# Windowed attention and gated layers of a decoder in one stage, batches interleaved, no stop between the two layers

## The chip, the cores and the metric

One NeuronCore of one Trainium2 chip runs the whole kernel. The metric is the device time of one execution in microseconds. The engines are PE (TensorE, matmuls and transposes), DVE (VectorE), ACT (ScalarE), POOL (GpSimd) and SP, which here only issues DMAs. Each takes its instructions in order; semaphores connect them.

## The reference, cut to what matters

The kernel computes a decoder on x (4 batches of 512 tokens, 256 channels): an RWKV layer, a quantised cross attention, a mixture of experts, a linear attention, a cross attention, and at the end two layers of windowed attention with a gated layer. Each of these blocks adds its result to x and normalises. The change is in the last block alone:

```python
def _layer(x, wqkv, qs, ksc, wo, lg, lb, w1, b1, w2, b2):
    h = shift_token(x)                     # second half of the channels comes from the token before
    q, k, v = jnp.split(h @ wqkv, 3, axis=-1)        # 8 heads of 64
    q = l2norm(q) * qs
    k = l2norm(k) * ksc
    q, k = rotary_xpos(q, k)
    o = local_attention(q, k, v)           # 128 queries see their own and the previous 128 keys
    x = x + o @ wo
    h = shift_token(x)
    h = (h - mu) / jnp.sqrt(var + 1e-05) * lg + lb
    a, g = jnp.split(h @ w1 + b1, 2, axis=-1)        # 682 hidden channels each
    return x + (a * gelu(g)) @ w2 + b2
x = _layernorm(x + layer1(layer0(x)))
```

## The kernel before, in words

`windowed` runs four stages one after another: attention of layer 0, gated layer 0, attention 1, gated layer 1. Each is a function that reserves its SBUF tiles and semaphores, makes a plan (a list of steps in one order), and then writes each engine's instructions by walking through that same plan. So the plan is the order of work on every engine. Between stages stands `settle`: every engine, SP too, waits for the last step of the stage.

**Attention** (`windowed_plan`, `attention_sp`, `attention_pe`, `attention_dve`, `attention_act`, `attention_pool`). A unit u is two windows of 128 tokens; a layer has 8 units, 16 windows (numbered 0 to 15 in this text, four to a batch). Weights and activations are split into a high and a low bf16 part, and a product takes three passes. Steps of a unit:

- `split`: ACT casts x, DVE shifts it by one token, POOL makes the low parts (L3034).
- `project`: 6 matmuls of 512 columns for q, k or v of a window (L2774); ACT copies the result out (L2972) and squares q and k (L2978); DVE sums the squares (L2875). `invert`: ACT takes the root (L2982), DVE the reciprocal.
- `rotate`: POOL multiplies by the sine (L3045, L3046), DVE by the cosine, adds POOL's part and multiplies by the norm (L2893, L2896, L2899). `turn`: 4 transposes on PE (L2783), a copy on ACT.
- `score`: mask products and q times k into banks 0 to 3 (L2795, L2802). `softmax`: DVE takes maxima (L2910), ACT the exponentials (L3008, which empties the banks), DVE the reciprocal sums and the weighting (L2916, L2919), each in two halves of four heads.
- `flip`: transposes of the weights (L2814), copied by DVE and ACT in turn (L2944). `combine`: weights times v (L2829), copy on ACT (L3020). `output`: times wo (L2839), DVE adds to x (L2930).

The plan puts the rotations of unit u+1 and the projections of unit u+2 among the scores, softmaxes, flips, combines and outputs of unit u. The first window of a batch looks at 128 keys only (`alone`), so its score, softmax and flips are half as large.

**Gated layer** (`ffn_plan`, `ffn_sp`, `ffn_pe`, `ffn_dve`, `ffn_act`, `ffn_pool`). The unit is a batch g. `normalise`: PE shifts the tokens (L3118, L3119), DVE takes statistics and scales (L3174, L3188), ACT the root (L3233); POOL adds the bias b2, and in layer 1 the x kept from the block's start, to x_tok (L3283, L3288). `transpose`: PE, then ACT scales (L3248), DVE makes high and low parts (L3198, L3200). `first`, six hidden tiles ft: 12 matmuls into two banks, value and gate (L3140); ACT gelu of the gate (L3257), DVE value times gate (L3209), ACT high part (L3262), POOL low part (L3304). `second`, two halves: 36 matmuls each (L3154), DVE adds to x_tok (L3217). `split1`, `split2` split w1 and w2 on ACT and POOL (L3237, L3241, L3292, L3296). At the end of layer 0, `channels` turns x into channel order for the next attention; in layer 1, `norm` is the final layer norm, and SP stores each batch.

All PSUM uses other than scores take banks 4 to 7 in rotation, in the order of the plan. A use waits until the one four uses before it is emptied:

```python
self.empty = m.emptied[bank], m.uses[bank]
...
use.update(m.banks(steps, (4, 5, 6, 7)))
```

## Time and profile before

| | us |
|---|---|
| median of 3 runs | 2854.57 (2853.91 to 2859.57) |
| profiled execution, its own time | 2848.74 |
| its span | 2847.4 |
| busy in the span: PE / DVE / ACT / POOL | 2229.3 / 1674.0 / 1182.0 / 566.6 |

The span is the time from the first to the last instruction in the profile; the execution's own time lies 1.3 us above it. Mean granted TensorE clock 0.876. The windowed block is the last 891 us. The page's forty slices of the span (71 us each) show it in the last twelve and a half:

```profile
PE   6993589896408999287589999995888697788678
...
DVE  4666965568763333466556565643777642677663
ACT  2222844345232333132225555553665442566442
POOL 2110000001363554401200000001222141322052
PEclk9996789998658999589689999997899898899999
```

### The profile page before, as it was taken

To read this page: it belongs to the slowest core of one execution; us is meant where nothing else is said; L and a number is where in the kernel's file an instruction comes from. 1 tells how busy PE (TensorE), PEld (TensorE's weight loads), DVE (VectorE), ACT (ScalarE), POOL (GpSimd) and SP (SyncE) were. 2 spreads that over 40 slices of the span, in tenths; PEclk is the share of its full clock that TensorE was granted. 3 is DMA by queue.
4 is the path that set the end of the run, shared out by engine and by line. 5 is a ranking of instruction groups with operands and counts; after the bars stand their busy time and mean duration, and the time that the engine had idled before them with its cause. 6 is when DMAs were issued, how large, how long until landed. Compare 5 with 4: busy or idle time off the path is not lost. (4 is left out here: it accounts for less than half of the span.)

```text
span 2847.4 us, 41664 instructions
## 1 busy us (share of the span) xinstructions
PE 2229.3 (78%) x15694; PEld 1432.6 (50%) x15694; DVE 1674.0 (59%) x3413; ACT 1182.0 (42%) x2185; POOL 566.6 (20%) x489
## 2 busy tenths in 40 slices
PE   6993589896408999287589999995888697788678
PEld 3552157573306888144235555653555444455534
DVE  4666965568763333466556565643777642677663
ACT  2222844345232333132225555553665442566442
POOL 2110000001363554401200000001222141322052
PEclk9996789998658999589689999997899898899999
DMA  3005000100360111323311111102000001000000
GB/s 109 1 1 155 14 1 1 45 1 1 96 215 26 46 46 38 108 65 79 102 48 36 24 36 24 24 13 88 1 1 1 11 1 59 1 1 1 36 12 23
DMA packets 75074, 113.30 MB, mean 40 GB/s; under 512 B 22916, under 2 KB 59744, under 8 KB 74208
## 3 DMA queue, kind: packets, MB, share of 16 engines
q1 hardware_dynamic: 71808, 102.24, 12.0%
q0 software_dynamic: 3072, 8.39, 0.9%
q8 instruction: 131, 2.15, 0.3%
q14 instruction: 63, 0.52, 0.1%
HBM read 85.38 MB, written 31.20 MB: 41 GB/s over the span
## 5 line engine op out<-in xcount | busy, mean ns | idle before, releaser
L2479 DVE TENSOR_REDUCE xa_max<-psum 128x1 f32<-128x1024 f32 (+1 forms) x256 | 248.8, 988 | 144.7 <-PE psum L2382 144.1
L2575 ACT ACTIVATE xa_work<-psum 128x1024 f32<-128x1024 f32 (+1 forms) x208 | 212.9, 1024 | 202.1 <-PE psum L2405 200.5
L2420 PE MATMUL psum<-xa_work,xa_values 128*33 128x128 f32 (+1 forms) x3328 | 232.1, 284 | 0.0
L2420 PEld LDWEIGHTS psum<-xa_work,xa_values 128*33 128x33 f32 (+1 forms) x3328 | 172.9, 114 | 78.9 <-issue 73.7
L2774 PE MATMUL psum<-wqkv_l,x_hl_l 128*128 128x512 bf16 x576 | 146.1, 401 | 60.6 <-POOL x_hl_l L3034 32.4
L3140 PE MATMUL psum<-h_ch_f,w_f 128*128 128x512 bf16 (+1 forms) x576 | 139.3, 400 | 32.1 <-DVE h_ch_f L3200 9.5
L1645 DVE TENSOR_SCALAR moe_raw<-psum,tile_b 128x256 f32<-128x256 f32 x184 | 78.3, 474 | 139.3 <-PE psum L1487 138.2
L2405 PE MATMUL psum<-xa_query_rows,xa_key_rows 98*128 98x512 bf16 (+1 forms) x416 | 131.5, 399 | 8.4 <-ACT xa_work L2575 7.7
L1741 POOL TENSOR_TENSOR x_ch<-moe_raw,x_ch 128x512 bf16<-128x512 f32 x92 | 105.5, 1158 | 149.9 <-ACT x_ch L1701 147.8
L1487 PE MATMUL psum<-moe_rows,moe_w 128*128 128x256 bf16 x1104 | 132.9, 279 | 3.0 <-POOL moe_rows L1737 3.0
L2382 PE MATMUL psum<-xa_key_rows,xa_query_rows 96*128 96x512 bf16 (+1 forms) x512 | 129.4, 348 | 6.7 <-DVE xa_max L2479 3.0
L1498 PE MATMUL psum<-moe_w,x_ch 128*128 x1104 | 130.2, 280 | 0.0
L3008 ACT ACTIVATE w_p_l<-psum,w_max_l 128x256 f32<-128x256 f32 (+1 forms) x256 | 110.6, 458 | 28.8 <-DVE w_max_l L2912 28.6
L2774 PEld LDWEIGHTS psum<-wqkv_l,x_hl_l 128*128 128x128 bf16 x576 | 56.0, 102 | 130.3 <-issue 48.6
L1487 PEld LDWEIGHTS psum<-moe_rows,moe_w 128*128 x1104 | 110.0, 100 | 18.8 <-issue 4.2
L1498 PEld LDWEIGHTS psum<-moe_w,x_ch 128*128 128x128 bf16 x1104 | 110.9, 101 | 16.7 <-issue 1.3
L3140 PEld LDWEIGHTS psum<-h_ch_f,w_f 128*128 128x128 bf16 (+1 forms) x576 | 56.8, 102 | 111.4 <-issue 33.9
L1038 PE MATMUL psum<-ctx_f,query_sum 128*128 128x512 f32 (+1 forms) x256 | 105.5, 538 | 7.9 <-DVE query_sum L1090 7.9
L3045 POOL TENSOR_TENSOR qk_other_l<-qk_raw_l,rotary_l 128x256 f32<-128x256 f32 x64 | 64.7, 1011 | 196.0 <-DVE qk_rot_l L2896 196.0
L1059 PE MATMUL psum<-ctx_f,probs_t_bn 128*128 128x128 f32 (+1 forms) x832 | 100.0, 277 | 2.8 <-DVE probs_t_bn L1116 2.8
L1701 ACT CAST x_ch<-moe_raw 128x512 bf16<-128x512 f32 x92 | 56.9, 618 | 101.4 <-DVE moe_raw L1645 101.4
L1174 POOL TENSOR_TENSOR x_tok<-x_tok,rows 128x4096 f32<-128x4096 f32 x1 | 8.8, 8809 | 451.5 <-DVE fused L1135 451.5
(439 smaller groups left out, 4832.2 us busy)
## 6 DMA issues: line engine op xcount, KB each, us to landing
xa_key_rows<-cross_keys SPq DMA_DIRECT2D x48, 200.1 KB, 3.5
moe_raw<-in_moe_w SPq DMA_DIRECT2D x16, 512.0 KB, 5.2
x_ch<-in_moe_w SPq DMA_DIRECT2D x16, 512.0 KB, 4.8
moe_rows<-slots_in SPq DMA_DIRECT2D x23, 256.0 KB, 2.8
slots_out<-moe_rows SPq DMA_DIRECT2D x23, 256.0 KB, 2.1
ctx_f<-in_ctxT SPq DMA_DIRECT2D x2, 2401.5 KB, 21.5
cross_keys<-xa_k_hl SPq DMA_DIRECT2D x6, 800.5 KB, 3.7
xa_query_rows<-cross_queries SPq DMA_DIRECT2D x48, 64.0 KB, 3.5
```

The lines of the kernel that those rows point to most:

```text
L1038: ins = pe.matmul(u.wide[:, c0 - a:c1 - a], t["qsum"][:, n * P:(n + 1) * P], t["keys"][:, b * S2 + c0:b * S2 + c1], start=True, stop=True)
L1487: ins = pe.matmul(u.ap[:, a * SLOT:(a + 1) * SLOT], w1[:, w, h, cf], t["x"][j % 2][:, x, h, :], start=(h, k) == (0, 0), stop=(h, k) == (1, 2))
L1498: ins = pe.matmul(u.ap[:, a * D:(a + 1) * D], t["hidden"][j % 2][:, x, f, q], w2[:, w, f, :], start=(f, k) == (0, 0), stop=(f, k) == (7, 2))
L1741: g.tensor_tensor(hidden[:, 1, f, :], t["act"][n % 2], hidden[:, 0, f, :], ALU.subtract).then_inc(*s.h_low.up())
L2382: ins = pe.matmul(u.wide[:, x - c0:y - c0], t["q_rows"][n % 3][0:SPLIT, a, qt * P:(qt + 1) * P], t["k_rows"][n % 3][0:SPLIT, a, x:y], star ...
L2405: ins = pe.matmul(u.wide[0:rows, a * T:(a + 1) * T], t["k_rows"][n % 3][:, a, kt * P:kt * P + rows], t["q_rows"][n % 3][:, a, :], start=Tr ...
L2420: ins = pe.matmul(total.ap[a * LANE:a * LANE + VC, c:c + PIECE], t["v"][b][0:rows, kt, first + a, :], exps[0:rows, a, c:c + PIECE], start= ...
L2479: v.tensor_reduce(t["maxes"][n % 2][:, qt * HU + a, part:part + 1], u.wide[:, 0:c1 - c0], AX.X, ALU.max).then_inc(*u.free)
L2575: act.activation(t["exps"][k % EXPS][0:rows], u.wide[0:rows].rearrange("p (m q) -> p m q", q=T), ACT.Exp, scale=1.0 / float(np.sqrt(np.flo ...
L2774: ins = pe.matmul(b.ap, x[:, i, h, w * P:(w + 1) * P], t["wqkv"][:, j, h, cols], start=(h, n) == (0, 0), stop=(h, n) == (1, 2))
L3008: ins = act.activation(t["p"][n % 2][:, i, lo:2 * P], scores[:, i, :], ACT.Exp, bias=t["peak"][n % 2][:, i:i + 1], scale=8.0, accum_out=t[ ...
L3140: ins = pe.matmul(u.ap[0:rows, :], t["w1"][:, y, h, o:o + rows], t["h_ch"][g % 2][:, x, h, :], start=(h, n) == (0, 0), stop=(h, n) == (1, 2))
```

## The change

The four stages of the block become one, with one plan of 545 steps for both layers.

- Units count on through both layers (0 to 15), batches too (g 0 to 7). `windowed_sp` walks the plan too.
- Gated steps of batch g (0 to 2 in a layer) stand among the windows of the next batches: `normalise` in window 4(g+1)+1, `root`, `scaled` and `transpose` in +2, hidden tiles 0 to 2 in +3, 3 to 5 in +4, `second` in +5, `channels` (layer 1: `stat`, `root_last`, `final`) in +6. So batch 0's are windows 5 to 10, batch 1's 9 to 14, batch 2's begin with window 13. What is not placed by window 15 comes after it, then batch 3. In layer 0 this rest is interleaved with `prologue(UPL)`: split, projections and rotations of layer 1's first unit and projections of its second.
- The weights of layer 1 are loaded by `fetch` steps: wqkv into the two buffers of raw q and k once the last units have read them, the rotary table, wo, w1, w2 as their readers finish. `weigh` and `tables` split and scale them.
- SBUF: one set of tiles for both layers. w_pt goes from two buffers to one, w_v from five to four, w_p from two buffers of eight heads to three of four heads, h_ch and hidden from two to one, h_act from three to two. The normalised tokens (h_tok before) are written into x_ch, in the batch's own part, which the attention has read by then; in layer 1 the kept x is loaded there, batch by batch. h_f32 and w_oc lie in the rows tile, raw w1 and w2 in the room of hidden and h_act.
- `normalise` copies the shifted half out of PSUM (DVE), and the scaling reads the copy. Semaphores of finals and statistics count once a batch.
- The first wqkv cast waits for its own half only.

The core of the diff:

```diff
+    early, late = {}, {}
+    for layer in range(2):
+        w0, g0 = layer * TILES, layer * B
+        late[w0] = [("split1", layer, 0)]
+        late[w0 + 1] = [("split1", layer, 1)]
+        late[w0 + 2] = [("split2", layer, n) for n in range(2)]
+        for g in range(g0, g0 + B - 1):
+            w = w0 + TPB * (g - g0 + 1)
+            for at, where, steps in ((1, late, [("normalise", g)]), (2, early, [("root", g), ("scaled", g)]), (2, late, [("transpose", g)]),
+                                     (3, early, firsts(g, 0, 3)), (4, early, firsts(g, 3, HT)), (5, early, seconds(g)[:1]),
+                                     (5, late, seconds(g)[1:]), (6, late, close(g))):
+                if w + at < w0 + TILES:
+                    where.setdefault(w + at, [])
+                    where[w + at] = where[w + at] + steps
+    swap = {TILES - 4: [("fetch", "wqkv", 0)], TILES - 2: [("fetch", "wqkv", 1), ("fetch", "tab", 1)]}
+    for w, steps in ((TILES - 3, [("weigh", 0)]), (TILES - 1, [("weigh", 1), ("tables", 1)])):
+        late[w] = late.get(w, []) + steps
+    plan, tail, last = prologue(0), [], []
+    for layer in range(2):
+        for u in range(layer * UPL, (layer + 1) * UPL):
+            main = []
+            for w in range(WU):
+                n = WU * u + w
+                main += swap.get(n, []) + [("score", u, w)] + tail[0:1] + [("softmax", u, w)] + early.get(n, []) + tail[1:2] + last
+                main += late.get(n, [])
+                last, tail = tail[2:], [("flip", u, w), ("combine", u, w), ("output", u, w)]
+            rotations = rotate(u + 1) if (u + 1) % UPL else []
+            projections = project(u + 2) if (u + 2) % UPL > 1 else []
+            plan += mingle(main, mingle(rotations, projections))
+        g = B * layer + B - 1
+        main = last + tail[0:1] + firsts(g - 1, 3, 4) + tail[1:2] + firsts(g - 1, 4, HT) + tail[2:] + [("fetch", "wo", 1)] * (1 - layer)
+        main += seconds(g - 1)[:1] + [("normalise", g)] + seconds(g - 1)[1:] + [("root", g), ("scaled", g)] + close(g - 1)[:1]
+        main += [("transpose", g)] + firsts(g, 0, 2) + close(g - 1)[1:2] + firsts(g, 2, HT - 1) + close(g - 1)[2:] + firsts(g, HT - 1, HT)
+        main += seconds(g) + [("fetch", "w1", 1), ("fetch", "w2", 1)] * (1 - layer) + close(g)
+        plan += main if layer else mingle(main, prologue(UPL))
+        last, tail = [], []
+    return plan
...
-                 v=ring("w_v", 5, [P, WU, INNER]), p=ring("w_p", 2, [P, HL, 2 * P]), pt=ring("w_pt", 2, [P, HL, 2, P]),
+                 v=ring("w_v", 4, [P, WU, INNER]), p=ring("w_p", 3, [P, 4, 2 * P]), pt=sb("w_pt", [P, HL, 2, P]),
...
-        settle(m, [use["output", UNITS_W - 1, WU - 1].done])
...
+            if what == "wqkv":
+                sp.wait_ge(*s.swung(4 * (UPL - 1 + h)))
+                sp.wait_ge(*s.swapped(4 * (UPL - 1 + h)))
+                sp.wait_ge(*s.squared(WU * (UPL - 1 + h)))
+                fetch_wqkv(1, h)
...
+        elif kind == "normalise":
+            b, x, late, st = use[step], batch_tokens(m, u), late_tokens(m, u), t["stats"]
+            v.wait_ge(*s.in_low(HALVES * WU * (u + 1)))
+            v.wait_ge(*b.full)
+            v.tensor_copy(late[:, :, :, P:D], b.ap.rearrange("p (h q d) -> p h q d", h=HALVES, q=2)).then_inc(*b.free)
...
+        elif kind == "first":
+            ft, = step[2:]
+            n, rows = HT * u + ft, hidden_rows(ft)
+            a, b = use[step + (0,)], use[step + (1,)]
+            if n > 1:
+                v.wait_ge(*s.h_low(n - 1))
...
+            act.wait_ge(*b.full)
+            act.activation(t["gate"][n % 2][0:rows, :], b.ap[0:rows, :], ACT.Gelu,
+                           bias=m.col("b1g", HT * (u // B) + ft, rows)).then_inc(*b.free)
+            if ft == 0 and u:
+                act.wait_ge(*use["second", u - 1, 1].full)
+            act.wait_ge(*a.done)
+            act.copy(t["hidden"][0:rows, 0, ft, :], t["act"][n % 2][0:rows, :]).then_inc(*s.h_high.up())
```

The order that results for windows 7 and 8 of layer 0 (numbers as in the code: u, w, then which or tile):

```
score(3,1) turn(4,0,0) flip(3,0) split(6) softmax(3,1) turn(4,0,1) first(0,0) project(5,1,1) first(0,1) turn(4,1,0) first(0,2) project(5,1,2) combine(3,0) turn(4,1,1) output(2,1) invert(5)
score(4,0) rotate(5,0,0) flip(3,1) project(6,0,0) softmax(4,0) rotate(5,0,1) first(0,3) project(6,0,1) first(0,4) rotate(5,1,0) first(0,5) project(6,0,2) combine(3,1) rotate(5,1,1) output(3,0) project(6,1,0)
```

## Rows read from the trace of the kernel before

**Rows 1.** Windows view: us, busy us (count) of PE, PEld, DVE, ACT, POOL; clock; DMA; GB/s.

```profile
1956.50:2256.00 299.50, 228.90 (x1600) 153.80 (x1600) 204.01 (x417) 166.36 (x435) 67.57 (x80) 0.88 0.06 21
2256.00:2398.50 142.50, 120.06 (x657) 65.32 (x656) 59.82 (x137) 52.03 (x74) 46.25 (x32) 0.93 0.02 6
...
2697.50:2847.40 149.90, 115.77 (x624) 61.35 (x622) 74.87 (x184) 57.00 (x79) 55.52 (x36) 0.92 0.09 33
2079.60:2234.50 154.90, 126.41 (x937) 89.56 (x936) 113.62 (x234) 91.17 (x249) 32.20 (x38) 0.91 0.00 1
```

**Rows 2.** PE timeline: start us, us, work; the mask products that open a score.

```profile
2079.58 1.91 PE L2795 MATMUL psum<-mask_b_l,ident_b_l 128*128 128x512 bf16 x4
...
2113.21 1.89 PE L2795 MATMUL psum<-mask_b_l,ident_b_l 128*128 128x512 bf16 x4
...
2130.22 0.60 PE L2795 MATMUL psum<-mask_b_l,ident_b_l 128*128 128x256 bf16 x4
...
2234.51 0.59 PE L2795 MATMUL psum<-mask_b_l,ident_b_l 128*128 128x512 bf16 x2
...
2446.64 0.60 PE L2795 MATMUL psum<-mask_b_l,ident_b_l 128*128 128x256 bf16 x4
...
2522.08 1.03 PE L2795 MATMUL psum<-mask_b_l,ident_b_l 128*128 128x512 bf16 x4
...
2675.01 0.59 PE L2795 MATMUL psum<-mask_b_l,ident_b_l 128*128 128x512 bf16 x2
```

**Rows 3.** Groups by line and form, 1970 to 2398.5 us.

```profile
L2774 PE MATMUL psum<-wqkv_l,x_hl_l 128*128 128x512 bf16 x288 | 72.8, 400 | 30.2 <-POOL x_hl_l L3034 16.4 <-ACT qk_raw_l L2972 9.6 <-ACT w_k_l L2991 3.0
L3140 PE MATMUL psum<-h_ch_f,w_f 128*128 128x512 bf16 x240 | 59.0, 405 | 12.8 <-issue 4.7 <-DVE h_ch_f L3200 4.6 <-DVE h_tok_f L3188 2.7
L3008 ACT ACTIVATE w_p_l<-psum,w_max_l 128x256 f32<-128x256 f32 x96 | 44.0, 485 | 13.0 <-DVE w_max_l L2912 13.0
...
L3045 POOL TENSOR_TENSOR qk_other_l<-qk_raw_l,rotary_l 128x256 f32<-128x256 f32 x32 | 32.4, 1011 | 99.2 <-DVE qk_rot_l L2896 99.2
...
L2910 DVE TENSOR_REDUCE w_max_l<-psum 128x4 f32<-128x1024 f32 x24 | 29.2, 1217 | 0.0
L3154 PE MATMUL psum<-w_f,hidden_f 128*128 128x256 bf16 x240 | 28.9, 273 | 0.0
...
L2893 DVE TENSOR_TENSOR qk_rot_l<-qk_raw_l,rotary_l 128x512 f32<-128x512 f32 x32 | 23.3, 728 | 0.0
L3304 POOL TENSOR_TENSOR hidden_f<-h_act_f,hidden_f 128x512 bf16<-128x512 f32 x20 | 23.1, 1157 | 51.3 <-ACT hidden_f L3262 51.3
...
L2944 DVE COPY w_pt_l<-psum 128x512 f32<-128x512 f32 x28 | 18.8, 686 | 11.0 <-PE psum L2814 10.4
...
L3209 DVE SCALAR_TENSOR_TENSOR h_act_f<-psum,cols,gelu_f 128x512 f32<-128x512 f32 x20 | 15.0, 749 | 39.4 <-ACT gelu_f L3257 35.9 <-issue 3.5
L3257 ACT ACTIVATE gelu_f<-psum,cols 128x512 f32<-128x512 f32 x20 | 13.8, 688 | 36.4 <-PE psum L3140 36.3
...
L3262 ACT CAST hidden_f<-h_act_f 128x512 bf16<-128x512 f32 x20 | 12.3, 618 | 18.3 <-DVE h_act_f L3209 18.3
```

**Rows 4.** Timeline of ScalarE: a table load and the exponential behind it.

```profile
2106.31 1.28 ACT L3008 ACT_TABLE_LOAD   x1 [2.75 <-DVE w_max_l L2912]
...
2107.61 0.47 ACT L3008 ACTIVATE w_p_l<-psum,w_max_l 128x256 f32<-128x256 f32 x1
```

**Rows 5.** PE timeline: an output step after idle time, and one without.

```profile
2092.78 3.62 PE L2839 MATMUL psum<-wo_l,w_oc_l 128*128 128x256 f32 x8 [2.76 <-ACT qk_raw_l L2972]
...
2107.32 1.89 PE L2839 MATMUL psum<-wo_l,w_oc_l 128*128 128x256 f32 x8
```

**Rows 6.** Timeline: GpSimd's weight split and the same VectorE subtraction beside it and alone.

```profile
2267.45 2.95 POOL L3292 TENSOR_TENSOR w_f<-w_f,w_f 128x1364 bf16<-128x1364 f32 x1
...
2267.81 3.13 DVE L3200 TENSOR_TENSOR h_ch_f<-h_f_f,h_ch_f 128x512 bf16<-128x512 f32 x1
...
2289.23 0.69 DVE L3200 TENSOR_TENSOR h_ch_f<-h_f_f,h_ch_f 128x512 bf16<-128x512 f32 x1
```

More of the change, by code:

```diff
@@ L2662, in rotate @@
         return steps + [("turn",) + o for o in order[-LAG:]]
-    plan = [("split", 0)] + project(0) + rotate(0) + project(1)
-    tail, last = [], []
-    for u in range(UNITS_W):
-        main = []
-        for w in range(WU):
-            main += [("score", u, w)] + tail[0:1] + [("softmax", u, w)] + tail[1:2] + last
-            last, tail = tail[2:], [("flip", u, w), ("combine", u, w), ("output", u, w)]
-        rotations = rotate(u + 1) if u + 1 < UNITS_W else []
-        projections = project(u + 2) if u + 2 < UNITS_W else []
-        plan += mingle(main, mingle(rotations, projections))
@@ L2674, in windowed_plan, with firsts, seconds, close @@
-    return plan + last + tail
+    def firsts(g, a, b):
+        return [("first", g, ft) for ft in range(a, b)]
+    def seconds(g):
+        return [("second", g, 0), ("second", g, 1)]
+    def close(g):
+        return [("channels", g)] if g < B else [("stat", g), ("root_last", g), ("final", g)]
+    def prologue(u):
+        return [("split", u)] + project(u) + rotate(u) + project(u + 1)
+    early, late = {}, {}
[12 more added lines that the diff above has]
+                    where[w + at] = where[w + at] + steps
@@ L2716, in windowed_attention @@
         for p in plan:
-            if p[0] in ("project", "turn", "combine", "output"):
+            if p[0] in ("project", "turn", "combine", "output", "normalise", "second"):
                 steps.append(p)
@@ L2720, in windowed_attention @@
                 steps += [p + (g,) for g in range(len(flips(*p[1:])))]
+            elif p[0] in ("transpose", "first", "channels"):
+                steps += [p + (i,) for i in range(2)]
             elif p[0] == "score":
@@ L2862, in attention_dve @@
         if kind == "split":
-            c0, first = u * WU * P, alone(u, 0)
+            c0, first = u % UPL * WU * P, alone(u, 0)
             if u:
                 v.wait_ge(*s.in_low(HALVES * u))
+            if u >= UPL:
+                for h in range(HALVES):
+                    v.wait_ge(*use["channels", (u - UPL) // WU, h].done)
             if first:
@@ L2954, in attention_act @@
         if kind == "split":
-            c0 = u * WU * P
+            c0 = u % UPL * WU * P
+            if u >= UPL:
+                for h in range(HALVES):
+                    act.wait_ge(*use["channels", (u - UPL) // WU, h].done)
             if u > 1:
@@ L3305, in ffn_pool @@
+            n, rows = HT * u + ft, hidden_rows(ft)
+            if ft == 0 and u:
+                g.wait_ge(*use["second", u - 1, 1].full)
+            g.wait_ge(*s.h_high(n + 1))
+            g.tensor_tensor(t["hidden"][0:rows, 1, ft, :], t["act"][n % 2][0:rows, :], t["hidden"][0:rows, 0, ft, :],
                             ALU.subtract).then_inc(*s.h_low.up())
```

629 lines of the change are left out of this document (320 added, 309 removed).

## The prediction, made blind

> **What bounds it now.** I read the stages first [rows 1]: of the 2847.4 us span the windowed part takes 890.9 us, from 1956.5 on. Attention of layer 0 lasts 299.5 us with TensorE (PE) busy for 228.9, its gated layer 142.5 with 120.1; layer 1 repeats the pair and ends with 149.9 for the gated layer, PE busy for 115.8. PE is the busiest engine in each and is idle for about 200 us in all, so filling that is the prize. Then I read the starts of the scores [rows 2], which cut attention into windows: each layer has 16, and windows 5 to 14 of layer 0 last 154.9 us (2079.58 to 2234.51), PE busy for 126.4 of them [rows 1]. From the score of window 15 to the first score of layer 1 there are 212.1 us (2234.51 to 2446.64): the attention tail, the gated layer, the stop and the start-up of layer 1. In layer 1 windows 5 to 14 take 152.9 us (2522.08 to 2675.01) and window 15 and the gated layer 172.4, to the end of the span.
>
> **What the change does.** No product is taken out. It moves, per layer, the gated steps of two batches, and the first half of the hidden tiles of a third, into windows 5 to 15; the rest of that batch and the last one come after window 15, in layer 0 interleaved with layer 1's start-up. In a cycle of four windows: D (7, 11, 15) gets three hidden tiles, A (8, 12) the other three, B (9, 13) both output products and the next normalise, C (6, 10, 14) root, scaling, transposes, channels. Price of the moved work on PE at full rate: a hidden tile is 12 matmuls. The mean of 405 ns in [rows 3] is latency, not spacing; 288 such matmuls are 72.8 us busy, 0.25 each, and steady groups come every 0.22, so a tile is 2.7 us. Half an output product is 36 matmuls at 0.12 (28.9 us for 240), 4.4 us. A normalise is 2 us, a transpose pair 1. For windows 5 to 14 that makes 12 tiles 32.2, 4 halves 17.6, the rest 10: 60 us. If nothing else stood in the way these windows would last 215 us or less.
>
> **Why I don't take 215.** All engines run in order and the moved steps share banks 4 to 7, in rotation, with the attention. I walked each window, with the durations of [rows 3]. Window 7, t=0 at the end of its score: PE turns and flips to 2.5; VectorE (DVE) copies two flip banks (0.69 each) to 3.2 and takes the first maximum (1.22, then 0.2 for the scaling) to 4.6; ScalarE (ACT) loads its table (1.28) [rows 4] and does eight exponentials at 0.47, to 9.7; DVE finishes weighting at 11.0. Meanwhile PE does a turn, tile 0 and a projection, to 7.1. Tile 1 then needs the turn's bank, which ACT copies only behind the exponentials, at 10.3: 3.2 us idle. Its second half needs the bank of tile 0's value, free after table load, gelu (0.69) and DVE's product (0.75), at 13.05. So it goes on: ACT's cast of a tile (0.62) waits for DVE's product, and every copy behind it waits too. The next score ends at 26.4 (it is a half-size one), against 17.0 measured [rows 2]. Window 8: tile 4's second half waits from 8.7 to 13.4, because DVE has the softmax and a rotation ahead of tile 3's product; then a POOL rotation (1.01+0.77) stands behind tile 4's low half (1.16) on GpSimd, DVE waits for it, tile 5's product behind that, and the output behind its ACT copy. 29 us, with the half-size softmax. The others in the same way. 9: the 4.4 us products stand where PE used to wait, 23.6. 10: DVE's list sets it (softmax to 12.7, rotation 14.8, scaling of the batch 18.2, rotation 20.3, a sum of squares, then the output's addition at 21.9, whose bank the transposes need), 25.7. 11: as 7 with one projection more, 27.7. 12: as 8 without projections; tile 5 waits for tile 3's product until 14.1, 23. 13: bound by PE, 19.8. 14: the output waits for its copy behind exponentials and root (10.2), the transposes for the scaling (13), 17. 5: the normalise on top of today's, 19.5. 6: the transposes wait for the scaling at 16, 21.2. Together 232.9 us. By the same walk today's window 7 is 15.5, where the rows say 17.0; so I add 1.5 per window: **248 us**, +93 against 154.9. The clock is one reason for the 1.5: after 2.76 us without work eight output matmuls took 3.62 us, elsewhere 1.89 [rows 5]; the mean granted clock of these windows is 0.91 of 2.4 GHz, so part of them ran at 1.2 [rows 1].
>
> **The border.** From the end of window 15's score: hidden tiles of batch 2 with flips, combine and outputs to 22.6, new weights and tables split on ACT and DVE beside it (their loads are issued two windows earlier, and SP has only waits ahead of them that are met by then), first projection at 26, second half of output product at 54.4. Then scaling of batch 3 stands on DVE behind rotations: PE idle for about 12 us until its transposes and casts are done at 69.9, then 35 us of tiles, projections and products; first score of layer 1 at 108. With the 2.8 of window 15's score that is 110.8 against 212.1: **-101.3 us**. This is the real gain: 14.5 us of weight loads, the latency of the gated layer's start and the start-up's idle time are covered.
>
> **The end of layer 1.** Same front; no start-up to mix in. Batch 2's products end at 47.2, transposes at 52.2, tiles 56 to 72.2, then 3.7 us idle for the last tile's gelu, product, cast and low half, products to 84.7, and statistics, scaling and store as today (7.5): 92, with some slow clock 95, and 2.8 for the score: 97.8 against 172.4, **-74.6 us**. But windows 5 to 14 of layer 1 cost 248 too, plus about 4.3 for the final normalisation on DVE in windows 10 and 14, against 152.9: **+99.4 us**.
>
> **Small edits.** Splitting w1 and w2 moves into windows 0 to 2: four ACT copies behind exponentials, four GpSimd subtractions. While such a one ran, a DVE subtraction with two SBUF inputs took 3.13 us instead of 0.69 [rows 6]. Bounds 0 and 10 us a layer; I take 4, since a rotation or two meets them: +8. The rings that shrink (w_pt to one, w_v to four, hidden and h_ch to one) cost 0: each is read out a window before it is written again, by PE's order of steps; if a combine were late by a window, the flip copies would wait for it, some 2 us each. Fetching batches of kept x on SP, one 0.5 MB load each, 0: the first reader, GpSimd, has a window until its next rotation. Waiting for each half of wqkv apart lets the first cast start earlier: -1.4. Table loads: counted over both orders of steps, 61 against 45; the walks have them in.
>
> **Sum:** 93 - 101.3 + 99.4 - 74.6 + 8 - 1.4 = +23 us. The profiled execution took 2848.7 us (span 2847.4); the median shown is 2854.6, 5.8 more. On the median: **2877.7 us**.
>
> **A rule beside the rows.** In [rows 4] a load takes 1.28 us and the exponential starts 0.02 later. The Trainium skill, ScalarE: Activation LUTs, What ACT_TABLE_LOAD costs, adds about 1.38 us of drain to each switch; by that the 16 extra loads would cost 22 us more, 2900 in place of 2878. The trace shows no such gap here, so I leave it out.
>
> **Rivals.** (1) *PE-bound filling, faster.* The tiles fit into today's waits because ACT and DVE reach them earlier than I walked; windows 5 to 14 then cost the 60 us of PE work alone: 33 less per layer, 66 in all, 2812; with half of today's 28 us of idle time filled as well, 2784. For it: ACT is busy for 91 and DVE for 114 of 154.9 us [rows 1], neither is full. Against it: order, not load, makes the waits. 0.36 for the whole side. (2) *GpSimd against DVE.* The 12 to 15 low halves (1.16 each) and bias additions of each layer now run beside rotations, which read two SBUF inputs. Some 52 us of GpSimd work in both layers; if each blocks DVE as in [rows 6] (2.44 of 2.95 us), +41: 2919. The Trainium skill, SBUF — State Buffer, Who interferes with whom, calls this an exclusive lock held for a whole instruction; the trace agrees with its 3.13 us. It decides if it hits DVE while PE waits for it. 0.12. (3) *The stop stays.* If layer 1's weight split (on ACT and DVE, behind window 15's tiles) or its load is late, the first projection waits as today, about 14.5 us: 2892. 0.05. My forecast: 0.41. The rest, 0.06, is terms that cancel to near zero.
>
> **Chances.** A measurement of this kernel tells 0.2% (6 us) from nothing. Faster 0.36, same 0.06, slower 0.58. Range: down to 2797, which leaves the deep end of rival 1 out, up to 2925, which takes in rival 2. The likeliest case's own range is 2850 to 2905 (1.4 us per window either way).
>
> **What would show it.** Right: score starts 23 to 30 us apart in windows 7 to 12 where they are 11 to 21 apart now; PE waiting there for gelu, for the tile's product and for copies behind exponentials; about 110 us from layer 0's last score to layer 1's first; 98 us from the last score to the end; some 60 table loads. Wrong: windows 5 to 14 in 215 us or less per layer (rival 1); rotations on DVE well above 0.73 us (rival 2); a hole of PE over 10 us before the first projection of layer 1 (rival 3).

## The result and the profile after

The changed kernel takes 2892.07 us (median of 4 runs, 2885.68 to 2895.47) against 2855.36 for the kernel before on the same chip: ratio 1.0123, 95% interval 1.0103 to 1.0144. The forecast was 2877.7, in a range of 2797 to 2925: the direction was right, the size some 14 us short (36.7 us slower in the medians, where 23 was forecast). The profiled execution shown here was the slowest of the four (2895.47, span 2894.2), and the one of the kernel before (2848.74) was faster than all its other runs, so the two profiles differ by 10 us more than the medians.

The windows view of the changed kernel, cut at the score starts: windows 0 to 4, windows 5 to 14, the border (score of window 15 to the first score of layer 1), the same three for layer 1, its last being the end. Columns as in [rows 1].

```profile
2005.60:2090.80 85.20, 64.85 (x425) 43.30 (x431) 61.97 (x121) 52.37 (x135) 31.54 (x30) 0.86 0.00 1
2090.80:2336.60 245.80, 188.70 (x1271) 123.80 (x1283) 154.44 (x338) 130.33 (x302) 51.64 (x55) 0.91 0.03 9
2336.60:2454.80 118.20, 93.75 (x538) 54.37 (x545) 50.75 (x98) 47.30 (x84) 29.43 (x30) 0.91 0.04 11
2454.80:2541.50 86.70, 63.89 (x425) 42.81 (x431) 62.03 (x122) 53.36 (x136) 30.32 (x29) 0.86 0.05 17
2541.50:2788.80 247.30, 190.89 (x1255) 122.33 (x1266) 159.39 (x354) 127.48 (x299) 56.77 (x57) 0.89 0.03 7
2788.80:2894.20 105.40, 77.09 (x436) 44.31 (x439) 41.32 (x102) 35.49 (x61) 21.50 (x16) 0.87 0.08 25
```

The stage of the kernel before, in the same cut, in two of its rows (windows 0 to 4 and the border of layer 0; windows 5 to 14 stand in [rows 1]):

```profile
2003.00:2079.60 76.60, 62.59 (x438) 40.37 (x437) 58.73 (x124) 49.39 (x133) 22.39 (x28) 0.91 0.00 1
2234.50:2446.60 212.10, 160.53 (x885) 89.33 (x884) 91.20 (x198) 79.10 (x132) 59.22 (x47) 0.88 0.06 24
```

So, between the same scores, in us:

| stretch | before | after | difference | forecast |
|---|---|---|---|---|
| to the first score | 2003.0 | 2005.6 | +2.6 | -1.4 |
| windows 0 to 4, layer 0 | 76.5 | 85.2 | +8.7 | +4 |
| windows 5 to 14, layer 0 | 154.9 | 245.8 | +90.9 | +93 |
| border | 212.1 | 118.2 | -93.9 | -101.3 |
| windows 0 to 4, layer 1 | 75.4 | 86.7 | +11.3 | +4 |
| windows 5 to 14, layer 1 | 152.9 | 247.4 | +94.5 | +99.4 |
| window 15 to the end | 172.4 | 105.4 | -67.0 | -74.6 |
| sum | | | +47 | +23 |

The spans differ by 46.8. Most of the first row is not the change's: the part of the program ahead of the stage is the same code, and its end lay up to 17 us apart between profiles (first score at 1993 to 2010 us), so everything below compares stretches, not spans. From the stage's first DMA to the first score it is 48.75 us before (1954.28 to 2003.03) and 48.21 after (1957.40 to 2005.61): the change takes 0.5 us off there, and the other 3.1 came from ahead of the stage. Two profiles of unaltered code differ by up to 2 us in a stretch, 4 in the end.

The reader should see two things in the first fence. In windows 5 to 14 PE is busy for 188.7 us where it was 126.4: 62 us more, close to the 60 of the forecast, which priced the moved work at full rate. But PE also idles 57.1 us there, where it idled 28.5. The holes were not filled, they doubled. And in windows 0 to 4 PE's work is unchanged while the stretch grew, with GpSimd busy for 31.5 us where it was 22.4.

**Inside window 7.** The timeline of the changed kernel, PE, ScalarE (ACT) and VectorE (DVE), from the softmax to the second half of tile 2 (the wait ahead of an instruction in brackets):

```profile
2144.82 1.28 ACT L3273 ACT_TABLE_LOAD   x1 [0.99 <-DVE w_max L3075]
2146.11 0.47 ACT L3273 ACTIVATE w_p<-psum,w_max 128x256 f32<-128x256 f32 x1
...
2149.72 0.63 ACT L3252 COPY w_k<-psum 128x512 f32<-128x512 f32 x1
2150.37 1.28 ACT L3323 ACT_TABLE_LOAD   x1
2150.41 4.57 PE L2986 MATMUL psum<-ff_ch,ff_w 128*128 128x512 bf16 x12 [4.16 <-ACT w_k L3252]
2151.66 0.69 ACT L3323 ACTIVATE ff_act<-psum,cols 128x512 f32<-128x512 f32 x1
2152.39 0.75 DVE L3142 SCALAR_TENSOR_TENSOR ff_act<-psum,cols,ff_act 128x512 f32<-128x512 f32 x1 [1.12 <-ACT ff_act L3323]
2153.17 0.62 ACT L3328 CAST ff_hidden<-ff_act 128x512 bf16<-128x512 f32 x1 [0.82 <-DVE ff_act L3142]
...
2157.38 1.47 PE L2986 MATMUL psum<-ff_ch,ff_w 128*128 128x512 bf16 x6 [0.67 <-DVE ff_act L3142]
```

This is the chain of the forecast step by step. The twelve matmuls at 2150.41 are tile 1: PE needs a bank whose copy (w_k) stands on ACT behind eight exponentials, and waits 4.16 us for it (walked, that is, worked out in the forecast: 3.2); then table load, gelu, product and cast of the tile before. After the wait the 12 matmuls take 4.57 us, against 2.7 at full rate. The forecast's second wait inside tile 1 doesn't show by itself: its bank is free at 2153.14, while the slow matmuls still run.

PE's groups in windows 5 to 14 of layer 0, changed kernel:

```profile
L2986 PE MATMUL psum<-ff_ch,ff_w 128*128 128x512 bf16 (+1 forms) x141 | 38.1, 422 | 19.0 <-DVE ff_act L3142 12.5 <-ACT w_k L3252 6.3
L2958 PE MATMUL psum<-wo,rows 128*128 128x256 f32 x80 | 22.9, 437 | 9.2 <-ACT w_k L3252 3.9 <-ACT w_q L3257 3.6 <-DVE ff_act L3142 0.9
L3000 PE MATMUL psum<-ff_w,ff_hidden 128*128 128x256 bf16 (+1 forms) x144 | 18.8, 284 | 0.0
...
L2973 PE MATMUL psum<-const,x_ch 128*128 128x128 f32 x24 | 5.9, 426 | 17.2 <-DVE x_ch L3121 11.3 <-DVE x_tok L3093 6.0
```

The gated layer's output products (`second`, L3000) wait for nothing. The hidden tiles (L2986) wait 19.0 us and the transposes (L2973) 17.2, for the tile's product, for copies behind exponentials, and for the scaling that stands on DVE behind softmax and rotations.

### The profile page after: what moved, and what is told of

Same layout as the page of the kernel before. It is cut to its first block and busy times, and to the rows that moved or that the text cites. A ratio compares the mean times of both kernels' runs of the same rounds, so it can differ in the third digit from the quotient of the medians.

```text
span 2894.2 us, 41751 instructions
## 1 busy us (share of the span) xinstructions
PE 2234.9 (77%) x15628; PEld 1441.2 (50%) x15694; DVE 1682.0 (58%) x3419; ACT 1202.5 (42%) x2201; POOL 562.2 (19%) x489
## 5 line engine op out<-in xcount | busy, mean ns | idle before, releaser
L2986 PE MATMUL psum<-ff_ch,ff_w 128*128 128x512 bf16 (+1 forms) x562 | 152.0, 426 | 60.4 <-DVE ff_act L3142 36.6
L2893 PE MATMUL psum<-wqkv,x_hl 128*128 128x512 bf16 x535 | 141.0, 404 | 35.3 <-POOL x_hl L3354 14.7
L2986 PEld LDWEIGHTS psum<-ff_ch,ff_w 128*128 128x128 bf16 (+1 forms) x576 | 59.4, 107 | 145.5 <-DVE ff_act L3142 45.5
L3273 ACT ACTIVATE w_p<-psum,w_max 128x256 f32<-128x256 f32 (+1 forms) x256 | 110.6, 458 | 15.6 <-DVE w_max L3075 15.4
L2893 PEld LDWEIGHTS psum<-wqkv,x_hl 128*128 128x128 bf16 x576 | 56.8, 103 | 104.4 <-issue 34.7
L3393 POOL TENSOR_TENSOR ff_hidden<-ff_act,ff_hidden 128x512 bf16<-128x512 f32 (+1 forms) x48 | 55.5, 1156 | 245.0 <-ACT ff_hidden L3328 245.0
L1059 PEld LDWEIGHTS psum<-ctx_f,probs_t_bn 128*128 128x128 f32 (+1 forms) x832 | 95.4, 192 | 3.4 <-DVE probs_t_bn L1116 3.4
```

The source lines that it names most:

```text
L1059: ins = pe.matmul(u.ap[:, 0:P], t["turned"][n % 2][0:rows, kt, :], t["values"][0:rows, n // TPB, kt, :], start=(kt == 0), stop=(kt == KT - 1))
L2893: ins = pe.matmul(b.ap, x[:, i, h, w * P:(w + 1) * P], t["wqkv"][:, j, h, cols], start=(h, n) == (0, 0), stop=(h, n) == (1, 2))
L2986: ins = pe.matmul(b.ap[0:rows, :], t["w1"][:, y, h, o:o + rows], t["h_ch"][:, x, h, :], start=(h, n) == (0, 0), stop=(h, n) == (1, 2))
L3273: ins = act.activation(t["p"][half % 3][:, i % 4, lo:2 * P], scores[:, i, :], ACT.Exp, bias=t["peak"][n % 2][:, i:i + 1], scale=8.0, accum ...
```

## The experiments

All durations are of windows views cut at score starts, as above. Every kernel ran on the same chip as the runs of the kernel before given with it.

### 1. One stage, but the gated layer behind the attention

The steps of batches are taken out of the windows, and run batch after batch behind window 15; in layer 0 all but batch 0 interleaved with layer 1's start-up. Buffers, code of each step and the splits among windows 0 to 2 stay as in the changed kernel.

```diff
-        for g in range(g0, g0 + B - 1):
-            w = w0 + TPB * (g - g0 + 1)
...
+        for g in range(g0, g0 + B):
...
+            part += (ready(g + 1) if more else []) + firsts(g, 3, HT) + ([("transpose", g + 1)] if more else []) + seconds(g)
...
-        plan += main if layer else mingle(main, prologue(UPL))
+            plan += main + rest[:cut] + mingle(rest[cut:], prologue(UPL))
```

> The changed kernel with no gated step inside the windows: all four batches' gated steps come after window 15, one batch after the other, in layer 0 interleaved with layer 1's start-up from batch 0's channels on. Same tiles, rings and weight loads. Theory 1 (the order of the moved steps among the attention, not the single stage, makes windows 5 to 14 long): they fall back from 246 and 247 us to 155 to 165 per layer; from layer 0's last score to layer 1's first it takes 185 to 200 us, the end 165 to 180; in all 2850 to 2875 us against 2892. Theory 2 (the single stage itself costs it: smaller rings, shared semaphores, x_ch reused): windows 5 to 14 stay above 200 us and the kernel stays above 2900.

Measured: 2865.29 us (2860.48 to 2866.97), before 2845.22, ratio 1.0070 (1.0046 to 1.0093).

```profile
1994.50:2082.30 87.80, 66.69 (x438) 43.83 (x437) 64.37 (x124) 52.73 (x136) 33.38 (x32) 0.86 0.00 1
2082.30:2235.50 153.20, 123.86 (x938) 88.45 (x937) 114.50 (x235) 92.68 (x251) 31.82 (x38) 0.93 0.04 15
2235.50:2435.20 199.70, 160.60 (x886) 89.39 (x885) 88.71 (x199) 76.44 (x130) 50.10 (x46) 0.91 0.02 7
...
2680.60:2859.20 178.60, 139.59 (x765) 78.25 (x763) 89.76 (x217) 61.22 (x103) 46.31 (x32) 0.90 0.08 24
```

Windows 5 to 14 return to 153.2 and 154.6 us. It is the gated steps among these windows, not the single stage and its buffers, that cost the 91 to 94 us. The border is 12.4 us shorter than before. That is the sum of several things: no stop, weights loaded ahead, the start-up mixed in, the splits gone from it, and another order of the gated steps. The end, which has no stop, got 6.2 us longer with the same order, so the single stage may be worth some 19 us in the border (an estimate, 12.4 and 6.2). Windows 0 to 4 stay long (87.8 and 90.8).

### 2. The cast of a tile later on ScalarE

The cast of each hidden tile is issued behind the next ACT step, so that its wait for DVE's product holds nothing up.

```diff
-            act.wait_ge(*a.done)
-            act.copy(t["hidden"][0:rows, 0, ft, :], t["act"][n % 2][0:rows, :]).then_inc(*s.h_high.up())
+            def cast(n=n, ft=ft, rows=rows, a=a):
...
+                pending.append(cast)
...
```

> The changed kernel with ScalarE's cast of a hidden tile (which waits for VectorE's product) put behind the next ScalarE step instead of right behind the gelu, except for a batch's last tile. If ScalarE standing in that cast's wait holds up the copies behind it, and with them the banks, windows 7, 8, 11 and 12 get 1 to 3 us shorter each and the kernel 8 to 20 us faster. If the value bank that waits for VectorE's product sets the pace, as the waits of PE say (36.6 us before the tile matmuls), under 5 us.

Measured: 2881.16 us in one run (before 2845.22); windows 5 to 14 take 245.9 and 248.7 us, no change beyond the 2 us spread. The forecast's remark that "every copy behind it waits too" is true in the timeline, and costs nothing that can be measured here. The end was 101.1, but experiment 5, whose casts stand as in the changed kernel, shows 101.3, so that is no gain either.

### 3. No table for gelu

Exp takes the place of Gelu in the hidden tiles, so those values are other ones; all else stays.

```diff
-            act.activation(t["gate"][n % 2][0:rows, :], b.ap[0:rows, :], ACT.Gelu,
+            act.activation(t["gate"][n % 2][0:rows, :], b.ap[0:rows, :], ACT.Exp,
```

> The changed kernel with Exp in the place of Gelu, so that this nonlinearity is another function than the reference's; nothing else differs. Exponentials and the gate share a table then: some 23 of 60 table loads go. If each such load (1.28 us) lies on the chain that sets a window, 20 to 30 us less. If the loads are hidden by other waits, under 8 us.

Measured: 2864.81 us in one run (before 2845.22). The table loads of ScalarE in the stage at the exponentials (L3273) and the gelu (L3323), changed kernel first, then this one:

```profile
L3273 ACT ACT_TABLE_LOAD x24 | 30.8, 1283 | 44.9 <-DVE w_max L3075 44.8
L3323 ACT ACT_TABLE_LOAD x13 | 16.7, 1283 | 17.6 <-PE psum L2986 17.4
```

```profile
L3273 ACT ACT_TABLE_LOAD x20 | 25.7, 1283 | 33.8 <-DVE w_max L3075 33.6
L3323 ACT ACT_TABLE_LOAD x3 | 3.8, 1283 | 17.6 <-PE psum L2986 17.6
```

Fourteen loads fewer, 60 to 46 in all (my expectation had counted on some 23). Windows 5 to 14 have six fewer each and take 236.8 and 238.5, 9.0 and 8.9 less: 1.5 us a load, with a spread of up to 2 us in each stretch. So nearly every load seems to lie on the path there, at about its own 1.28 us. With 2.66 us for each switch, the 1.28 and the 1.38 of drain that the Trainium skill states (ScalarE: Activation LUTs, What ACT_TABLE_LOAD costs), six on the path would have given 16 us; this run doesn't agree. Nor does the timeline of window 7 above: the copy of w_k ends at 2150.35, the load starts at 2150.37, and the gelu 0.01 us behind its end. The loads explain a tenth of the 91 us.

### 4. The smaller rings, on the kernel before

```diff
-                 v=ring("w_v", 5, [P, WU, INNER]), p=ring("w_p", 2, [P, HL, 2 * P]), pt=ring("w_pt", 2, [P, HL, 2, P]),
+                 v=ring("w_v", 4, [P, WU, INNER]), p=ring("w_p", 3, [P, 4, 2 * P]), pt=sb("w_pt", [P, HL, 2, P]),
...
```

> The kernel before with the changed kernel's attention rings alone: w_pt one buffer instead of two, w_v four instead of five, w_p three half buffers instead of two whole ones. The prediction took them at 0. If that holds, the span stays within 2 us of 2847 and windows 0 to 4 at 75 to 77 us a layer. If the rings are what makes windows 0 to 4 of the changed kernel last 85.2 and 86.7 us, they do so here: 8 to 10 us a layer, 16 to 40 us in all.

Measured: 2849.36 us in one run, before 2845.22. Windows 0 to 4 take 76.6 and 77.5 us, windows 5 to 14 154.8 and 154.1, border 212.1, end 172.6. Each is within 2.1 us of the kernel before; these three rings cost nothing, as priced. Those of the gated layer (h_ch, hidden, h_act) were not tried by themselves.

### 5. The changed kernel almost without the low splits

The low parts of w1 and w2 are made for eight columns of each piece only and no longer read (PE reads the high part in their place), so this part of the precision is left out. ScalarE's four casts stay.

```diff
-                        ins = pe.matmul(b.ap[0:rows, :], t["w1"][:, y, h, o:o + rows], t["h_ch"][:, x, h, :],
+                        ins = pe.matmul(b.ap[0:rows, :], t["w1"][:, 0, h, o:o + rows], t["h_ch"][:, x, h, :],
...
-            g.tensor_tensor(t["w1"][:, 1, h, :], t["w1_f32"][:, h, :], t["w1"][:, 0, h, :], ALU.subtract).then_inc(*s.w1_low.up())
+            g.tensor_tensor(t["w1"][:, 1, h, 0:8], t["w1_f32"][:, h, 0:8], t["w1"][:, 0, h, 0:8], ALU.subtract).then_inc(*s.w1_low.up())
...
```

> The changed kernel without the low parts of w1 and w2: GpSimd's four subtractions a layer are cut to 8 columns and the three passes of the gated products read the high part in their place, so that the number of matmuls is the same; the output lacks the low parts' share. If GpSimd against VectorE makes windows 0 to 4 long (85.2 and 86.7 us), they fall to 77 to 79. If the order of steps does, they stay above 82.

Measured: 2872.65 us in one run (before 2850.8). Windows 0 to 4 fall from 85.2 and 86.7 to 78.2 and 79.7, 7.0 in each layer; windows 5 to 14 stay (245.8 and 245.6). The collision in the changed kernel's timeline, then the group of the first rotation in windows 0 to 4 of layer 0, changed kernel:

```profile
2056.22 2.61 POOL L3377 TENSOR_TENSOR ff_w<-ff_act,ff_w 128x1280 bf16<-128x1280 f32 x1 [10.23 <-ACT ff_w L3301]
2056.89 2.48 DVE L3056 TENSOR_TENSOR qk_rot<-qk_raw,rotary 128x512 f32<-128x512 f32 x1
```

```profile
L3056 DVE TENSOR_TENSOR qk_rot<-qk_raw,rotary 128x512 f32<-128x512 f32 x10 | 10.8, 1079 | 0.0
```

and the same group in this experiment:

```profile
L3056 DVE TENSOR_TENSOR qk_rot<-qk_raw,rotary 128x512 f32<-128x512 f32 x10 | 7.3, 731 | 0.0
```

### 6. Two tiles a window, not three

```diff
-                                     (3, early, firsts(g, 0, 3)), (4, early, firsts(g, 3, HT)), (5, early, seconds(g)[:1]),
-                                     (5, late, seconds(g)[1:]), (6, late, close(g))):
+                                     (3, early, firsts(g, 0, 2)), (4, early, firsts(g, 2, 4)), (5, early, firsts(g, 4, HT)), (6, early, seconds(g)[:1]),
+                                     (6, late, seconds(g)[1:]), (7, late, close(g))):
...
```

> The changed kernel with two hidden tiles in each of three windows instead of three in two, output products and closing one window later. Three tiles in a row make PE wait twice for a value bank that VectorE frees only behind its softmax; two need all four banks once. By that theory windows 5 to 14 get shorter by 5 to 15 us a layer. If what counts is the number of windows with a table change and a broken-up softmax, they get longer, by 0 to 8 us a layer.

Measured: 2888.55 us in one run (before 2850.8), 37.8 us slower than before, as slow as the changed kernel. Windows 5 to 14: 244.0 and 243.6, 1.8 and 3.8 less, with batch 1's closing step now in window 15, behind them, and the border 1.4 longer; a miss for the theory that three tiles in a row are what hurts. The rival, that such windows get longer, is not borne out either. Spreading brings nothing that is clear of the spread.

### 7. Tiles ahead of the softmax

```diff
-                main += swap.get(n, []) + [("score", u, w)] + tail[0:1] + [("softmax", u, w)] + early.get(n, []) + tail[1:2] + last
+                main += swap.get(n, []) + [("score", u, w)] + tail[0:1] + [p for p in early.get(n, []) if p[0] == "first"] + [("softmax", u, w)] + [p for p in early.get(n, []) if p[0] != "first"] + tail[1:2] + last
```

> The changed kernel with one thing moved: in windows 7, 8, 11 and 12 the hidden tiles placed there stand ahead of the window's softmax on every engine, not behind it. Theory (a tile's bank and its product are held up because ScalarE and VectorE reach the gelu and the product only behind the exponentials and the weighting): the tiles run without those waits, PE waits for ff_act less than the 36.6 us of the changed kernel's stage, but the softmax, and with it the flips, come later; windows 5 to 14 change by -15 to 0 us per layer. Rival (the softmax chain itself sets these windows, so whatever is put ahead of it is added): windows 7, 8, 11 and 12 grow by 3 to 6 us each, windows 5 to 14 to 258 or more per layer.

Measured: 2887.6 us in one run (before 2850.57). PE's group of the hidden tiles over the whole stage, changed kernel, then this one:

```profile
L2986 PE MATMUL psum<-ff_ch,ff_w 128*128 128x512 bf16 (+1 forms) x562 | 152.0, 426 | 60.4 <-DVE ff_act L3142 36.6 <-ACT w_k L3252 9.9 <-DVE ff_ch L3133 6.5
```

```profile
L2986 PE MATMUL psum<-ff_ch,ff_w 128*128 128x512 bf16 (+1 forms) x561 | 134.7, 390 | 27.3 <-DVE ff_act L3142 14.0 <-DVE ff_ch L3133 6.5 <-issue 3.5
```

The tiles' waits fell by 33 us and their busy time by 17, and yet windows 5 to 14 took 243.2 and 245.2, only 2.6 and 2.2 less, and the kernel was as slow as the changed one (37.0 us above the kernel before). The wait has moved to the mask products that open the next score, which need the banks that the exponentials empty. Changed kernel, then this one:

```profile
L2914 PE MATMUL psum<-mask_b,ident_b 128*128 128x512 bf16 (+1 forms) x128 | 36.8, 416 | 6.4 <-ACT w_p L3273 6.4
```

```profile
L2914 PE MATMUL psum<-mask_b,ident_b 128*128 128x512 bf16 (+1 forms) x128 | 41.7, 447 | 38.3 <-ACT w_p L3273 38.3
```

Window 7 shrank from 27.7 to 23.5, window 8 grew from 26.7 to 32.7. The theory has the waits right, and the rival (258 us or more) is wrong in its size, but its reason holds in part: the tiles run freely, and what they save, the score behind the later softmax pays. The waits named in a group say where time is spent, not what it is worth to remove them.

### 8. Experiment 1 with the attention's own order

The splits had also changed how the attention steps are interleaved with projections and rotations. Here they are put in after the interleaving, so that the attention has exactly the order of the kernel before.

```diff
-        late[w0] = [("split1", layer, 0)]
-        late[w0 + 1] = [("split1", layer, 1)]
-        late[w0 + 2] = [("split2", layer, n) for n in range(2)]
...
+        for score, steps in ((("score", u, 1), [("split1", layer, 0)]), (("score", u + 1, 0), [("split1", layer, 1)]),
+                             (("score", u + 1, 1), [("split2", layer, n) for n in range(2)])):
...
```

> e1_serial_one_stage (no gated step in the windows) with the four weight-split steps put into the plan after the mingling, so that the attention's steps of windows 0 to 3 stand in exactly the order of the kernel before; the splits themselves stay in these windows. e1 took 87.8 and 90.8 us for windows 0 to 4 where the kernel before took 76.5 and 75.4. If the longer list has moved the turns, projections and rotations among each other and that costs it, windows 0 to 4 come back to 77 to 81 us, and the kernel is 15 to 25 us faster than e1 (2845 to 2852). If it is GpSimd's subtractions against VectorE, they stay at 86 or more.

Measured: 2861.78 us (2858.98 to 2869.45), before 2850.80, ratio 1.0039 (1.0025 to 1.0053). Windows 0 to 4: 85.5 and 87.1, where 77 to 81 was expected if the order is what costs, and 86 or more if GpSimd's subtractions are. The order is worth 2.3 and 3.7 us against experiment 1; the rest of their growth is elsewhere.

### 9. Experiment 8 with another order of gated steps

The next batch's normalise stands between this batch's hidden tiles rather than in front of all that are left, and the last batch's closing steps stand behind all hidden tiles, ahead of the output products.

```diff
-            if g > g0:
-                part += firsts(g, 0, 2) + close(g - 1)[:1] + firsts(g, 2, 3) + close(g - 1)[1:]
-            part += (ready(g + 1) if more else []) + firsts(g, 3, HT) + ([("transpose", g + 1)] if more else []) + seconds(g)
...
+            part += [norm] + firsts(g, 3, 4) if g == g0 else firsts(g, 0, 1) + [norm] + firsts(g, 1, 4)
+            part += [root, scaled] + firsts(g, 4, HT) + ([("transpose", g + 1)] if more else [])
+            part += (close(g - 1) if g > g0 else []) + seconds(g)
...
```

> e8_serial_order_kept with another order in the gated part: normalise of the next batch after the first hidden tile, root and scaling after the fourth, closing steps of the batch before in front of the output product. In e1 PE waited 4.05 us per batch for VectorE's product behind the scaling, and 2.5 to 3.5 us for the last low half. If that is the gated part's loss against the kernel before (178.6 us from the last score to the end, 172.4 there), the end falls by 6 to 14 us and the stretch from layer 0's last score to layer 1's first (199.7 in e1) by 4 to 12: then this version beats the kernel before by 5 to 20 us. If the single hidden buffer is what costs it, both stay within 3 us.

Measured: 2840.27 us (2836.86 to 2843.29), before 2850.80, ratio 0.9965 (0.9952 to 0.9977). The border falls from 199.6 to 184.5 us (4 to 12 less was expected), the end from 178.6 to 168.5. So the single hidden buffer, the rival of this expectation, is not what held them up.

### 10. Experiment 9 with the splits at windows 14 and 15

No rotation runs there, since the layer's last unit has been rotated.

```diff
-        for score, steps in ((("score", u, 1), [("split1", layer, 0)]), (("score", u + 1, 0), [("split1", layer, 1)]),
-                             (("score", u + 1, 1), [("split2", layer, n) for n in range(2)])):
-            at = plan.index(score)
+        for step, steps in ((("softmax", u + UPL - 1, 0), [("split1", layer, n) for n in range(2)]),
+                            (("softmax", u + UPL - 1, 1), [("split2", layer, n) for n in range(2)])):
+            at = plan.index(step) + 1
```

> The version with the gated layers behind the attention (e9), with one thing moved: the splits of w1 and w2 stand behind the softmax of windows 14 and 15 of each layer, where no rotation runs on VectorE, not before the scores of windows 1 to 3. Theory (the splits on GpSimd hold VectorE's rotations, some 7 us per layer): windows 0 to 4 fall from 85.5 and 88.3 to 78 to 80, near the 76.5 and 75.4 of the kernel before; windows 5 to 14 gain 0 to 2 us, border and end 0 to 3; in all 10 to 15 us less than e9, ratio to before some 0.992. Rival (the time is lost to the four casts on ScalarE or to the order of steps, wherever they stand): windows 0 to 4 keep 82 or more, or windows 14, border and end grow by as much as is gained, and the ratio stays at 0.9965.

Measured: 2819.93 us (2806.43 to 2823.06), before 2850.57, ratio 0.9897 (0.9881 to 0.9912). This beats both kernels. Its profiled execution is its fastest (2806.43), so only stretches are compared:

```profile
1993.40:2068.80 75.40, 59.87 (x430) 39.23 (x436) 58.35 (x124) 48.95 (x132) 22.35 (x28) 0.93 0.00 1
2068.80:2220.80 152.00, 122.06 (x927) 88.05 (x936) 113.67 (x235) 92.68 (x250) 31.82 (x38) 0.93 0.04 15
2220.80:2408.20 187.40, 154.98 (x874) 89.37 (x884) 92.13 (x199) 80.17 (x134) 59.17 (x48) 0.92 0.03 7
2408.20:2485.10 76.90, 59.93 (x431) 39.35 (x437) 58.42 (x125) 49.88 (x133) 21.27 (x27) 0.93 0.06 21
...
2638.50:2805.10 166.60, 131.77 (x756) 75.77 (x763) 90.08 (x218) 67.73 (x109) 55.14 (x36) 0.92 0.08 26
```

```profile
L3065 DVE TENSOR_TENSOR qk_rot<-qk_raw,rotary 128x512 f32<-128x512 f32 x10 | 6.8, 677 | 0.0
```

Windows 0 to 4 fall by 10.1 and 11.4 us, below even the range expected (78 to 80), to 75.4 and 76.9: the level of the kernel before. Windows 5 to 14 take 152.0 and 153.4. The border takes 2.9 us more than in experiment 9, the end 1.9 less. So the splits cost 10 us a layer where experiment 9 had them and almost nothing in the windows without rotations; the whole kernel gained some 20 us, where 10 to 15 was expected. Experiment 5 says that 7 of the 10 are GpSimd's subtractions. The other 3 may be the four casts on ScalarE, for which GpSimd still waits there, or, in the changed kernel, the attention's shifted order (2.3 and 3.7 us in experiment 8); no run separates these.

## Why the prediction was right, and by how much not

**The PE-bound filling (rival 1)** is out: 245.8 and 247.4 us against its 215. No engine is full there (PE 188.7, DVE 154.4, ACT 130.3 of 245.8 us), which fits the reason given against it, that order and not load makes the waits. Which wait in that order costs the time is not shown: in experiments 2, 3, 6 and 7 each suspected one was removed or moved by itself, and that gave 0 to 9 us of the 91.

**Windows 5 to 14** were the step that carried the forecast: 248 walked, 245.8 measured, and 252.3 against 247.4 in layer 1. Some of that closeness is luck: the walk itself gave 232.9, 1.5 us a window was added from one window of today, and errors of single windows cancel. Window by window, the walks with their 1.5 us gave 21.0, 22.7, 27.9, 30.5, 25.1, 27.2, 29.2, 24.5, 21.3, 18.5; the scores are 21.7, 24.0, 27.7, 26.7, 25.5, 27.9, 27.8, 23.6, 24.1, 16.7 apart. Window 8 was walked 3.8 too long. Window 13 was called "bound by PE" and is not: its output step waits 3.60 us for ACT's copy of w_q, so it came out 2.8 longer. And the lengths came true although the waits that the walk names are not worth their own length: experiments 2 and 7 took two kinds of them away.

**The border** was forecast at 110.8 and took 118.2, a term mis-sized by 7.4. PE's largest waits there in the changed kernel:

```profile
2352.34 4.19 PE L2986 MATMUL psum<-ff_ch,ff_w 128*128 128x512 bf16 x12 [4.94 <-DVE ff_act L3142]
2403.48 1.97 PE L2973 MATMUL psum<-const,x_ch 128*128 128x128 f32 x8 [6.80 <-DVE x_ch L3121]
2412.77 4.48 PE L2986 MATMUL psum<-ff_ch,ff_w 128*128 128x512 bf16 x11 [6.47 <-DVE ff_ch L3133]
```

The last two are the 12 us hole of the walk (13.3 measured). The first is a wait the walk didn't have, and the tiles behind each hole ran 1.5 and 1.8 us slower than the 2.7 assumed. **The end** was forecast at 97.8 and took 105.4 in this profile, 100.4 to 103.9 in the other interleaved ones; it has waits of the same kind, 8.7 us for tiles' products and 5.5 for the last low halves, where the walk had 3.7. In the border I priced tiles behind a hole at full rate; the end had an allowance for slow clock of 3 us.

**The stop (rival 3)** is gone: no hole of 10 us before the first projection of layer 1, which starts at 2367.56, 2 us later than walked. That the measured 2892 is just the number that rival 3 gave is chance; its mechanism did not occur. The rest of the border's 93.9 us is mostly not cover but transfer, as the comparison with experiment 10 shows, which has the same products in series. There border and end take 187.4 and 166.6 us. The changed kernel's windows 5 to 14 hold the tiles and output products of two batches of four (and the normalise and transposes of a third). That saves 69.2 and 61.2 us in border and end, and costs 93.8 and 94.0 in the windows: a batch costs some 47 us among the attention and 31 to 35 behind it. The hidden premise of the change, that a gated layer in series leaves PE holes worth covering, fails: in experiment 10's border PE is busy for 155.0 of 187.4 us. "This is the real gain", I wrote of the border; only 24.7 of its 93.9 us are more than transfer (212.1 against 187.4), and experiment 10 has them without the interleaving.

**The splits** were the worst-sized term: 4 us a layer, with 0 to 10 as bounds; measured 8.7 and 11.3 with all else in those windows, and 10.1 and 11.4 by experiment 10 against 9. "A rotation or two meets them" is right as far as it goes: in each layer two rotation products ran beside a long subtraction, at 2.13 and 2.48 us where 0.68 is usual. What the forecast left out is what follows. GpSimd comes late to its own rotation products, VectorE's next steps wait for them (1.38 and 0.69 us) or run beside them, at 1.09 to 1.13 us instead of 0.69. VectorE's three rotation instructions took 1079, 873 and 826 ns in the mean, against 677, 692 and 692 in experiment 10, some 7 us over ten rotations (731, 782 and 794 in experiment 5, so not all of it is the subtractions). That is rival 2's mechanism, real but in another place and at a third of its price by experiment 5 (14 us in both layers): its 41 us (52 at 2.44 of 2.95 us make 43) were to come from low halves and bias additions too. In windows 5 to 14 the second rotation does run at 928 ns where it was 714, but what this costs there was not tried by itself. The rule of the Trainium skill, SBUF — State Buffer, Who interferes with whom, agrees with the 2.48 us rotation beside the 2.61 us subtraction.

**The rest:** rings at zero is confirmed by experiment 4 for the attention's; some 60 table loads were forecast and 60 counted; no added drain fits experiment 3. The earlier first cast came 2.1 us sooner after the loads were issued (4.7 us against 6.8), but the first score only 0.5 us sooner, where 1.4 was forecast. Terms too small by 7.4, 7.6, 4.7 and 7.3, and window terms too large by 2.1 and 4.9, with 4.0 up to the first score (3.1 of it from ahead of the stage), make up the difference between +23 and +47 in the profiles. The forecast of the medians came closer than its terms, because 10 of the 47 us are in the choice of the two profiles.

What stays open: no single wait accounts for the 57 us of idle PE time in windows 5 to 14. The runs exclude the cast's wait, the number of tiles per window and their place before or behind the softmax as the main cause, and give table loads 9 us of the stretch; I take the rest to be the serial chain through ACT and DVE that most of these windows now have twice, which is argued, not shown.

## What to carry to other kernels

Before interleaving two stages to fill idle time, put each in its best serial order and see how much idle time is left. Here the serial order with one stage, reordered batches and splits moved out of the rotations' way took 1.0% off the kernel, where the interleaving added 1.2%. In this kernel the in-order engines share banks, and no engine is full in a window; work added to the windows lengthened them by more than its own duration: 62 us of PE work made 91. And try a long two-input GpSimd operation where VectorE has no two-input operations of its own; the same four subtractions and casts cost 10 us a layer among rotations and almost nothing elsewhere.

## What the hardware showed that I had not expected

- A GpSimd subtraction that began 0.67 us ahead of a VectorE rotation kept its length (2.61 us; 2.64 in experiment 10 with no rotation beside it), while the rotation took 2.48 us where 0.68 is usual. It is not always VectorE alone that pays. Right behind it both are longer than the 0.73 and 0.69 us that they take by themselves:

```profile
2058.79 1.17 POOL L3365 TENSOR_TENSOR qk_other<-qk_raw,rotary 128x256 f32<-128x256 f32 x1
2059.41 1.09 DVE L3059 TENSOR_TENSOR qk_rot<-qk_rot,qk_other 128x512 f32<-128x512 f32 x1
```

- It is not the splits alone. A bias addition of the gated layer does the same in window 6 (timeline of the changed kernel), and itself takes 2.73 us against a mean of 2.34 in experiment 10:

```profile
2132.16 2.73 POOL L3381 TENSOR_TENSOR x_tok<-x_tok,rows 128x1024 f32<-128x1024 f32 x1 [2.21 <-DVE x_ch L3121]
2132.72 2.72 DVE L3059 TENSOR_TENSOR qk_rot<-qk_rot,qk_other 128x512 f32<-128x512 f32 x1
```

- Six table loads fewer made windows 5 to 14 9 us shorter, 1.5 us a load where a load lasts 1.28 (the difference is within the spread of a stretch). PE's own work there got shorter too: 1284 matmul records are busy for 186.9 us in experiment 3, and 1283 for 190.4 in experiment 2, at a mean granted clock of 0.93 and 0.91.
